# Attention mega-kernel: global scores as 64-row products over zero rows, rows loaded head by head, and a new merge order

## What is computed (reference, cut to what matters)

```python
h = _layernorm(x) * (1 + ca) + sa
q = (h @ Wq + bq).reshape(b, 16, 8, t)      # a plain reshape of [512, 128]
k, v = ...                                  # the same
attn = softmax(einsum('bhdt,bhds->bhts', k, v) * temperature)
out = einsum('bhdt,bhts->bhds', q, attn)
x = x + ga * out.reshape(b, t, d)
h = _layernorm(x) * (1 + cb) + sb
x = x + gb * ffn(h)      # two layers, 8 heads, windows of 64 rows
```

## Time and profile before

| | |
|---|---|
| median of 3 runs | 1280.28 us (1274.93 to 1286.37) |
| the profiled execution, its own time | 1273.49 us |
| span, first to last instruction | 1271.4 us |
| mean granted PE clock | 0.908 |
| PE, DVE, ACT, POOL busy | 82%, 74%, 73%, 40% of the span |
| stream a | first score product at 37.4 us, last at 638.4 us |

### The profile page before, as it was taken

How to read it: one execution, slowest core, us unless ns; L and a number is a source line. 1 busy time by engine, 2 the same in 40 slices (tenths; PEclk the granted TensorE clock), 3 DMA queues, 4 the chain that set the end, 5 groups by cost and what they waited for, 6 DMA issues and landing times.

```text
span 1271.4 us, 23838 instructions
## 1 busy us (share of the span) xinstructions
PE 1046.8 (82%) x8124; PEld 524.9 (41%) x8124; DVE 946.8 (74%) x1945; ACT 922.3 (73%) x2782; POOL 504.1 (40%) x577
## 2 busy tenths in 40 slices
...
PEclk8687889897888888968888999999899999998999
...
GB/s 209 138 132 36 101 43 106 28 67 82 16 97 45 34 117 13 88 58 19 1 9 30 31 1 30 31 10 38 30 2 1 47 23 9 31 30 1 31 31 17
DMA packets 24647, 59.15 MB, mean 47 GB/s; under 512 B 2832, under 2 KB 3024, under 8 KB 23376
## 3 DMA queue, kind: packets, MB, share of 16 engines
...
## 4 chain that ended last, share of the span: by engine, by line
PE 41%; DVE 30%; ACT 14%; issue 6%; POOL 4%; DMA 3%; SPq 1%; ACTq 0%; DVEq 0%; POOLq 0%
DVE neg_max L1151 8%; PE psum L494 6%; PE psum L445 5%; ACT E L866 5%; PE psum L550 4%; PE psum L569 4%; PE psum L436 4%; PE psum L540 4%; ACT rot_work L960 4%; DVE rot_work L1218 3%; DVE work L1214 3%; DVE ss L1222 3%; PE psum L575 3%; PE psum L529 2%; PE psum L519 2%
## 5 line engine op out<-in xcount | busy, mean ns | idle before, releaser
L866 ACT ACTIVATE E<-psum,neg_max 128x512 f32<-128x512 f32 x512 | 347.3, 704 | 85.0 <-DVE neg_max L1151 63.1
L1151 DVE TENSOR_REDUCE neg_max<-psum 128x2 f32<-128x1024 f32 x256 | 308.2, 1214 | 80.3 <-PE psum L436 78.0
L786 POOL TENSOR_TENSOR work<-work,rot_work 128x512 f32<-128x512 f32 x128 | 162.7, 1272 | 159.5 <-DVE rot_work L1218 159.2
L436 PE MATMUL psum<-v_rows,k_rows 32*128 32x512 f32 x512 | 135.0, 554 | 96.2 <-ACT E L866 56.7
L799 POOL TENSOR_TENSOR rot_work<-rot_work,rz 128x512 f32<-128x512 f32 x128 | 132.7, 1042 | 183.5 <-DVE rz L1245 183.4
L960 ACT ACTIVATE rot_work<-psum,neg 128x128 f32<-128x128 f32 x512 | 182.8, 394 | 29.9 <-DVE neg L1240 16.0
L494 PE MATMUL psum<-wqkv_sb,hs 128*128 128x512 f32 x384 | 188.7, 620 | 9.6 <-DVE hs L1208 4.3
L445 PE MATMUL psum<-E,qz 128*32 128x512 f32 x1024 | 160.8, 705 | 2.5 <-POOL qz L764 2.5
L764 POOL TENSOR_TENSOR qz<-qT,rz 128x32 f32<-128x32 f32 x128 | 31.0, 242 | 329.7 <-DVE rz L1155 317.1
L436 PEld LDWEIGHTS psum<-v_rows,k_rows 32*128 32x128 f32 x512 | 53.0, 205 | 247.9 <-issue 133.0
L794 POOL TENSOR_TENSOR work<-work,rn 128x512 f32<-128x512 f32 x128 | 133.0, 1052 | 28.7 <-DVE rn L1110 28.4
...
## 6 DMA issues: line engine op xcount, KB each, us to landing
...
k_scr<-hi SPq DMA_DIRECT2D x16, 256.0 KB, 3.0
k_scr<-lo SPq DMA_DIRECT2D x16, 256.0 KB, 3.4
v_scr<-hi SPq DMA_DIRECT2D x14, 256.0 KB, 3.1
v_scr<-lo SPq DMA_DIRECT2D x14, 256.0 KB, 3.4
...
```

Of the source, the lines that this page charges most:

```text
L436: pe.matmul(bank, k_rows[r:r + 32, hh, P * j:P * (j + 1)], v_rows[r:r + 32, b % 2, hh, :], start=True, stop=True).then_inc(full, 1)
L786: pool.tensor_tensor(qk[s][:, i, w, :], qk[s][:, i, w, :], sinp[s][:, n % 2, :], ALU.add).then_inc(rot_sum[s], 1)
L866: act.activation(E[:, (b * NG + g) % E_RING, 2 * half + m, :], pair[:, m], ACT.Exp, bias=neg_max[:, n, m:m + 1], accum_out=z[:, n, m:m + 1 ...
L1151: dve.tensor_reduce(neg_max[:, n, :], pair, AX.X, ALU.max, negate=True).then_inc(max_ready, 1)
```

## The change

1. Each score product runs over 64 rows. `k_rows` gets a second half (index w = q // 2): in half w only the blocks of two values of q hold data, the other two groups of partitions hold zeros. Block q always lies in group GROUP_OF[q], so that partitions 0 to 63 hold q = 0 and 2, and 64 to 127 hold q = 1 and 3. A product over 64 rows of k and v then adds the wanted block and a block of zeros. POOL clears all of `k_rows` once at the start (semaphore `s_kzero`).
2. Every block is loaded by a DMA of its own (32 rows of 2 KB): 16 for k and 16 for v in a batch. The v rows are issued head group by head group, each a step of SP's stream a. In batch 0, ACT issues v of group 0 only, and SP issues k and v of the groups in turn.
3. ORDER and BANKS are new for all engines.

```diff
-PIECES = [[(q, n, (q + hh) % HQ) for q, n in ((0, HQ - hh), (HQ - hh, hh)) if n] for hh in range(HQ)]
+GROUP_OF = [0, 2, 1, 3]
...
     "SP": (
-        "aaaaaaaaaaaaaaxaaaaaaaaaaaaaaxaaaaaaxaaxaaaaaaaaaaaaaxxxyxyxyxyxyxyxyxyxy"
+        "aaaaaaaaaaaaaaaaaaaaaaxaaaaaaaaaaaaaaaaaaxaaaaaaaaaaxaaxaaaaaaaaaaaaaaaaaaxxxyxyxyxyxyxyxyxyxy"
...
-            k_rows = sa("k_rows", [P, HQ, T], F32R)
+            k_rows = sa("k_rows", [P, 2, HQ, T], F32R)
...
-        def rows_in(eng, dst, scr, hh, landed):
-            for q, m, r in PIECES[hh]:
-                eng.dma_start(dst[32 * r:32 * (r + m)].bitcast(F32),
-                              scr[q:q + m, hh].rearrange("q t d s -> q (t d) s")).then_inc(landed[hh], 16)
+        def rows_of(scr, q, hh):
+            return scr[q, hh].rearrange("t d s -> (t d) s")
+
+        def values_in(eng, b, hh):
+            for q in range(HQ):
+                r = 32 * GROUP_OF[q]
+                eng.dma_start(v_rows[r:r + 32, b % 2, hh].bitcast(F32), rows_of(v_scr, q, hh)).then_inc(v_in[hh], 16)
+
+        def keys_in(eng, hh):
+            for q in range(HQ):
+                r = 32 * GROUP_OF[q]
+                eng.dma_start(k_rows[r:r + 32, q // 2, hh].bitcast(F32), rows_of(k_scr, q, hh)).then_inc(k_in[hh], 16)
...
-                    r = 32 * ((2 * half + m + hh) % HQ)
-                    pe.matmul(bank, k_rows[r:r + 32, hh, P * j:P * (j + 1)], v_rows[r:r + 32, b % 2, hh, :],
+                    r = 2 * 32 * m
+                    pe.matmul(bank, k_rows[r:r + 64, half, hh, P * j:P * (j + 1)], v_rows[r:r + 64, b % 2, hh, :],
...
-            def a_values_in(b):
+            def a_values_in(b, hh):
                 passed(sp, v_out, (b + 1) * 16 * 4)
-                for hh in range(HQ):
-                    rows_in(sp, v_rows[:, b % 2, hh], v_scr, hh, v_in)
+                values_in(sp, b, hh)
...
+                if b == 0 and hh == 0:
+                    sp.wait_ge(s_kzero, 1)
+                keys_in(sp, hh)
...
             for hh in range(HQ):
+                if hh:
+                    a_values_in(0, hh)
                 a_keys_in(0, hh)
...
+            pool.memset(k_rows[:].rearrange("p w q t -> p (w q t)").bitcast(F32), 0.0).then_inc(s_kzero, 1)
...
             def values_first_in():
                 passed(act, v_out, 16 * 4)
-                for hh in range(HQ):
-                    rows_in(act, v_rows[:, 0, hh], v_scr, hh, v_in)
+                values_in(act, 0, 0)
```

More of the change, by code:

```diff
@@ new lines @@
+        "aaxxxaaxaaaaaxxaaxaaaaxaxaaaaaxaaaaaxaxxxxxxaaaxaaaaxaaaaaaaaxaxxxaxaaxxxaaaaxxxaaxaaxaaaaxxaaxaaaaa"
+        "xxxxaaaaaaxaaxaxxaaaxaaxxxaxaaaaaxxxaxaaxaxxaaxaaaxaaaaaaaaaaxaaaaaaxaaaxxxxxxaaaaxaaaaaxxxxxxaxaaxx"
+        "xxaxaaaaaxaxxaaxaaaaxaxaxxaaaaaaaaaaxaaaxxaaaxxxxaxaaaaxxaxxaaxaxxaaaxaxaaaxaaaaaxxxxaaaxxxxaaaaaxaa"
+        "aaxxxxxxxxxxxxxyxyyxyyyyyyyyyyxxxxxxxxyxyxxxyxyxxyxxyxyyxxxyyxxyyyyxyyyyyxyxyxxyyxxxxyyxxyxxxxxxxxxx"
+        "yyyyyyyxxyxxxxxxyyxxyyyyxyyyyyxxxyxyyxxxxyxyyxyxyxyxyxyyxyyyyyyxxxxxxxyyxyyxyyyyxyxxxxxxxxxyxxyyyyyy"
@@ L92 @@
-        "yyyyxxyxyxxyyyyy"
+        "aaaaaaaaaaaaaaaaaaaaaaaaaaaaaaaaaaaaaaaaaaaaaaaaaaaaaaaaaaaaaaaaaaaxaaaaaaxaaaaaaaaaaaaaaxaaaaaaaaaa"
+        "aaaaaaaaaaaaaaxaaaxaaaxxaaxxaxxxaaaxaaxaxaaaaaaaaaaxaaaaaaxxaaxaxxxaaaxaxxaaxxxaaaaxxxaaxaxaaxaaxaaa"
+        "aaxaaaaaxaxaaaxaxaaaaaaaaaaaaxxxaaaaaaxaxaaaaaxxxxaxaaaxxxaaxaxxaaxaaaaaaaxaaaaaaaaxxxxaxxxxxaaxxxaa"
+        "axxxaxxaaaaaaxxaaaaaxaaxaxaaaxaxaaaaaxxxaaaxaaaaaaxaxaaxaaaaaxaaaxaxaaxaxaaxaxaxaxaaaaxaxxaaxaaaaaaa"
+        "aaxaaxxaaxxxxxaaaaxxxxaxaaaaaxxxaaxxaxaaxaaxaaaaaaxaaaaaaaxaxaaxaaaaaaaxxaxaaaxaxaaaxxaaaxxaaxxaxxax"
@@ new lines @@
+        "aaaaxxaxaaaaaaxaaaaaaaaaaaaxxaaxaxaxxxaaxxxxaxaaaxxaaxxxaxaaxaaxaaxxaxaaxaaaaaaaaxxxxaaaaaaxxaxayxyx"
+        "xxxxxxxyxxyxyxyyyyxyxxyxxyxxxyyyxxxxxxxxxxyxxyyxyyyyyxxyyxyyyxyyyyyyyxxxxxyyyxyxyxxxxxxyyxxyxxyyxyxx"
+        "xxyxxyxyyyyyxxxxyxyxyxyxxxxxyxyyyxxyyyxyyyxyyyyyxxxyyyxyxxyyxyyxyxxyxxxxxxyyyxyxyyxyxyyyyxyxxyyxxxxy"
+        "yxxxyyxxxyyxxxxxyxxyyxyyyyyxxyxyyyxyyyyyyxxxyxxyxyxyyyxxyxxxxxxyxyxyyyxyxxxxyxxyxyyxxyxxxyyxxyyxxxyx"
+        "yxyxyyyxxyyyxyyyxyyyyyxxxyyyxyxyxyxyyxyxyxxxxxxxxyyyxyxyyxyyxyyyyxyxyxxxxyyxyxxyyxxxxyxxxxxxyxyyyyyy"
@@ new lines @@
+        "axxxxaaaaaaaaxaaxxxaxxaxxxaaaxxaxxxaxaxaaxaaxaxaaaxaaaaaaxxxyxxxxxxxxxxxyxyxyyyyyxxxyyyyxyxxxxxyyxxy"
+        "xxxxyyyyxxxxyyxxyxxyyxxyyyyxyyyyxyyyxyyyxyyxyxxxxxyxxxxyxxyxxxxxyxxxxxxyyxyyxyyxyyyxxyyxyyxxxxxyyyyx"
+        "yxyxyxyxyyyxyyyyxyyxyyyxyyyyyxxyxxyxxxxxxxyxxxyxxyxxxxxyyxxyyyyxyyxyyyxxyyxxxxyxyxxyxyyyxxyyxyyxyxxy"
+        "yyyxyyyyxyyxyyxyyxyyxxxyxxxxyxxxxyxxyxxxxxxyxxxyyxyyxyyxyxxxyyyxxyyxxyxxxxyyyyxyyxyyyyyxyyyyxyyxyyyx"
+        "yyyyyxxyxxyxxxxxxxxxyxxyxxxxxxyxyxyxxyyyyyyyyyxxyyxyxxxyxxyyyxxxyxyxxyyxyxyyyyyxyyyxyyyxyxyyyxyyxxxy"
@@ L113 @@
+        "xxxxxxyxyxyxyxyxyyyxyyyxyxyyyyyyyyyyyyxxxxxxxxxxxxxxxxyyyyyxxyyyxxyyyxyxyyxyxyyyyyyyyyxxxxxxxxxxxxxx"
+        "yxyyxyyyyyyyxxyxyyxyyyxxyxyyyxyyyy"
     ),
     "SP": (
[L115 removed]
+        "aaaaaaaaaaaaaaaaaaaaaaxaaaaaaaaaaaaaaaaaaxaaaaaaaaaaxaaxaaaaaaaaaaaaaaaaaaxxxyxyxyxyxyxyxyxyxy"
     ),
@@ L258, in build @@
         s_silexp, s_sil, s_setup = sem("s_silexp"), sem("s_sil"), sem("s_setup")
-        s_gcol, s_tables, s_clamp, s_qz = sem("s_gcol"), sem("s_tables"), sem("s_clamp"), sem("s_qz")
+        s_gcol, s_tables, s_clamp, s_qz, s_kzero = (
+            sem(n) for n in ("s_gcol", "s_tables", "s_clamp", "s_qz", "s_kzero"))
         s_chain = sem("s_chain")
```

99 lines of the change are left out of this document (40 added, 59 removed).

## The result

| | before | after |
|---|---|---|
| median of the comparison (4 runs each) | 1282.74 us (1274.93 to 1286.37) | 1258.83 us (1254.97 to 1260.61) |
| ratio after / before, 95% interval | | 0.9836 [0.9805, 0.9868] |
| profiled execution | 1273.49 us, span 1271.4 | 1260.61 us, span 1258.6 |
| mean PE clock of the span | 0.908 | 0.937 |

The change made the kernel 1.6% faster, 21 us by the ratio. The forecast was 1257 us and 23 us less than before. The two profiled executions lie only 12.9 us apart: that of the kernel before was 9 us faster than its median in the comparison, that of the kernel after 2 us slower.

A forecast was written before the change was run, and what follows sets the result against it. No engine alone bounds the kernel (PE busiest, 82%); row waits and PE's clock in stream a can be won. 5 + 7 + 15 - 4 = 23 us off 1280.28 gives 1257; range 1232 to 1283.

The forecast's parts named there:

- the likeliest case: Whole kernel: the forecast itself, 23 us gained, 1257 us; chance 0.60.
- the signs: Whole trace: first product near 33 us, no batch 1 or 6 wait over 1, issues 0.5, clock 0.92, stream a by 625.
- start, from smaller pieces: Batch 0's v_rows loads: small pieces use more DMA engines, first exponential earlier; 5 us gained, bounds 0 and 7.
- later loads: Row loads of later batches: waits before batches 1 and 6 go; 7 us gained, bounds 1 and 8.
- zeroes: POOL's memset of k_rows at the start: hidden in POOL's idle time, cost 0; without that cover 3.8 us.
- products, shared row groups: Score products on PE: a second pair must follow the first, some 26 times in 256; 4 us lost, bounds 0 and 10.
- clock, by 64 rows: PE in stream a: half of 171 us at 1.2 GHz go; 15 us gained, bounds 0 and 29.
- order: PE's merge order: stream x starts 24 us later, batch 1 loses what next batches get; 0, bounds -10 and +24.
- a first score product near 33: Start of stream a: first score product near 33.0 us instead of 37.40.
- Rival C: Row loads: 32 issues a batch at 0.75 us each keep the later waits, start gains 3; 1274 us, chance 0.09.
- rival A: PE clock: stays as it is or its gain stays off the chain; 1272 us, chance 0.19.
- Rival B: Batches 1 to 3: delayed stream x makes them together over 12 us longer; 1292 us, chance 0.12.

The follow-up runs named there:

- e4: Kernel before with the new small-piece loads alone (32-row products, old order, no zeroes): 1266.76 us, ratio 0.9890.
- e10: The same kernel as e4, run again on the chip of e9: 1265.05 us, ratio 0.9899.
- e7: Kernel after, with POOL's memset of k_rows made to wait for the end of DVE's setup: 1256.04 us, ratio 0.9824.
- e8: Kernel after, with the old ORDER and BANKS and the memset of k_rows behind DVE's setup: 1251.66 us, ratio 0.9786.
- e3: Kernel after with the ORDER and BANKS of the kernel before (64 rows, new loads, zeroes): 1255.95 us, ratio 0.9811.
- e9: e4 with every pair of 32-row products reading the same two row groups (scores not the reference's): 1264.93 us, ratio 0.9902.
- e1: Kernel after with score products over 32 rows again, same loads, zeroes, order and banks: 1272.64 us, ratio 0.9959.
- e6: Kernel after with data in place of zeroes on all 64 rows (scores not the reference's): 1256.16 us, ratio 0.9827.
- e2: Kernel before with the new ORDER and BANKS alone (32 rows, old large pieces): 1293.34 us, ratio 1.0108.
- e5: Kernel after with score products over all 128 rows (scores not the reference's): 1265.73 us, ratio 0.9905.

## Why the prediction was right, and where it was not

The time came out at 1258.83 against 1257, in the likeliest case and well inside the range. Of the signs, stream a was over by 618.4 us (forecast 625) and the clock and the issues held; two did not, as said below. The terms, one by one:

| term | forecast | measured |
|---|---|---|
| start, from smaller pieces | 5 us gained | 6.9 to the first exponential (e4) |
| later loads | 7 gained | not measured alone; loads as a whole 12 to 14 (e4, e10), forecast 12 |
| zeroes | 0 | 3.6 lost at the first product; at the end 1.5 by the ratios and 3.3 of span (e7 against after), 3.2 by the ratios (e8 against e3), each within the intervals |
| products, shared row groups | 4 lost | 0, give or take some 5 (e9 against e10) |
| clock, by 64 rows | 15 gained | 13 (e8 against e4) to 16 (after against e1) |
| order | 0 | 3 to 5 lost (e3 against after, e8 against e7) |
| sum | 23 gained | 21 gained |

**The start.** The mechanism was as forecast: with pieces of four blocks the DMA share was 0.28, with pieces of 32 rows 0.58. The size was put too low: from the first issue to the first product the forecast had 5.4 us (2 for the issues, 3.4 for landing), and 3.8 (e4) to 4.0 passed. The time that the step named, a first score product near 33, was missed (35.15), and that was not the loads' doing: in e4 and e7, where nothing delays the issue, it was 31.3 and 31.5.

**The zeroes: the step that was wrong.** "Cost nothing; without that cover 3.8." The step looked for POOL's own work behind the memset and found 11 us of idle time, which was true. It did not look at what other engines did beside it. DVE's TENSOR_SCALAR lasted until the memset was over (4.89 to 8.78), and DVE's setup is on the path to the first product. The hint stood in the trace of before: the same instruction took 0.80 us there beside POOL's smaller memsets, the next on the same tile 0.20. The Trainium skill ("SBUF — State Buffer", section "Who interferes with whom") says that VectorE and GpSimd share a pair of SBUF ports as an exclusive lock, that a tensor_scalar can run in a mode that takes it, and that the loser blocks for the whole instruction; the trace agrees, with 3.89 us beside a memset of 3.50 and 0.44 without it (e4). The page also gives the pair to whichever issues first; here the instruction that began at 4.89, beside the memset of qz, was held through the one of k_rows too, which began at 5.25. That POOL's memset was the cause, e7 and e8 show: one wait in front of it, and the instruction takes 0.80 and 0.77 us again. The price that the forecast gave for a missing cover, 3.8, was near the 3.4 by which the setup shifted.

**Later loads.** The loads as a whole came out in size. Issues were at 0.42 us in the median and 0.55 for the v pieces of batch 1 (forecast 0.5), landing 1.9 us (3.4). That the seven k issues of before, 13.10 us, were held by few busy DMA engines fits the fourteen small ones, which took 6.39. The sign to look for, "no wait of over 1 us before the first product of batch 1 or 6", held for batch 1 (0.75) and not for batch 6 (1.86), where the wait is now for ACT and no longer for the rows. Rival C, issues of 0.75 us, is out.

**The products.** The forecast counted 26 pairs of 256 that start beside the one before; there were 17. Every pair that had started beside the one before now follows it, as forecast, but of "half of it on the chain: 4 us lost" nothing is seen in e9. Twice the rows did not lengthen a product (median 497 and 496 ns).

**The clock.** Forecast: half of 171 us at 1.2 GHz go, 0.92 or above. Measured: 85 us of 171 are left, 0.93. The half was a choice without a row behind it, and no row showed 64 rows in place of 32, so that it came out this close is luck. That 64 rows are the cause is shown by e1, that zeroes are as good as data by e6, and that the shared row groups are not the cause by e9. The price of 15 us for 85 us less of slow clock fits the 13 to 16 us measured. The scatter of one kernel gives about the same, as an estimate: over the 13 executions of the kernel before on the chip of e1 to e4 the time fell by 5.4 us for each 0.01 of mean clock, which makes 15 us of the 0.028 between e4 (0.907 in the mean of its executions) and e8 (0.935). Here the rule of the Trainium skill that was weighed ("TensorE: Matmul & The Clock Gate", "What's actually happening"), a clock set by how busy the engine has been, falls short for this kernel: in batch 1 the clock was 0.75 with 45.38 us of PE busy time in 55 and 0.97 with 37.08 in 52. Had it held, the time would have been rival A's, 1272; e1, the kernel after with 32 rows, measured 1272.64; that the two agree to a microsecond is partly chance, since e1 also bears the losses of zeroes and order.

**The order.** Forecast nothing, bounds -10 to +24. Alone in the kernel before it cost 14 us (e2): batch 2 waited 6.74 us for its rows, and the part behind stream a grew by 10 us. With the small pieces it cost, as an estimate, 5 to 7 us at 32 rows (e1 against e4 and e10, less the memset's share) and 3 to 5 at 64. Rival B's sign, batches 1 to 3 together over 12 us longer, was 8.8 us longer in e2 (218.1 to 226.9 us) and 6.6 us shorter in the kernel after (211.5): a loss of B's kind was there with the old loads, and with the new loads at the same 32 rows it is gone: 218.8 us in e1. The 6.74 us of waiting for rows account for most of it; that none of it was crowded engines is not shown.

Two errors of some 3 us to the bad (zeroes, order) stood against one of up to 4 to the good (products) and 2 at the start; the sum owes a part of its closeness to that.

**Where the rest went.** Stream a became 18 us shorter (601.0 to 583.2) and started 2.2 us earlier, and the part behind it grew by 7.2 us (633.0 to 640.2): 12.8 us of span, between the two profiled executions. By e3 and e8 (635 to 636 with the old order) 4 to 5 of the 7.2 us would be the order's; but single profiled executions of one order differ by nearly as much (636.5 to 640.2 among e6, e7 and the kernel after). What the length of this part follows in all twelve traces is its own time at 1.2 GHz: 633.0 us with 49 us of it (before), 635.1 to 636.9 with 55 to 59 (e1, e3, e4, e6, e8, e9, e10), 640.2 with 66 (after, e7), 641.8 with 79 (e5) and 642.8 with 83 (e2). So the growth may be the clock's, and what part of it the order brings is not shown.

**Still open.** Whether and how the new order brings more time at 1.2 GHz into the part behind stream a; what makes products over 32 rows lower the clock; and whether e8's lead over e3 is the memset alone (0.9786 and 0.9811, intervals overlap; the spans differ by 7.3 us, more than the 3.5 that the memset can give).
